# One core: local attention with the norm of z taken out of the ring, its normalisation on POOL, the reciprocals one step earlier, and a new order of the entry of layer 0

## The chip, the cores and the metric

The kernel runs on one NeuronCore of one Trainium2 chip. The metric is the time of one execution on the device in microseconds (us); lower is better. The engines are PE (TensorE: matrix products and transposes, results to PSUM), DVE (VectorE), ACT (ScalarE), POOL (GpSimd, which reads and writes SBUF only) and SP (SyncE, which issues the DMAs). Each engine runs its own instructions strictly in the order in which they are written; between engines there are only semaphores.

## The reference, cut to what matters

Two batches of 1024 tokens, 128 features. First a gated linear attention (chunks of 64), a norm and an addition; its output is normalised again and is the input of a transformer of two layers. The change lies in those layers, and in how the first of them begins beside the end of the linear attention. In each layer, for each token:

```python
h = shift_token(x)                      # half of the features taken from the token before
q, k, v = split(h @ wqkv)               # 8 heads of 64
q = l2norm(q) * qs ; k = l2norm(k) * ksc
q, k = rotary_xpos(q, k)
sim = q @ k.T                           # own window of 64 tokens and the one before, masked
o = softmax(sim) @ v
x = x + o @ wo
h = shift_token(x)
h = (h - mean(h)) / sqrt(var(h) + 1e-05) * lg + lb      # this is z
a, g = split(h @ w1 + b1)
x = x + (a * gelu(g)) @ w2 + b2
```

## The kernel before, in words

All tensors are float32, apart from the masks of the scores. The 2048 tokens are 16 tiles of 128 tokens (NT = 16; tiles n and n + 1 of a pair belong to the two batches). The linear attention works on 8 pairs of tiles (NP = 8). Its last four pairs run interleaved with the first tiles of layer 0; the order of this stretch is written out by hand for each engine in `attention_beside_last_pairs` (POOL L512, PE L1017, ACT L1434, DVE L1976). From tile FREE_TILE = 3 on, in layer 1 from tile 0 or 1 on, all engines run a loop `iterate(engine, step)`, in which a step k issues a fixed list of stages, each for the tile k + lag. These lists (`step` on POOL L507, `attn_step` on PE L981, ACT L1410 and DVE L1941) are the only thing that sets the order of the work, and four or five tiles are under way at once. A layer's end (`drain`) puts the last stages between the blocks of the feed-forward part, which takes groups of four tiles and needs their z.

For one tile the stages follow each other like this, over the engines:

- PE transposes the tile (L865), ACT copies it into h (L1334, L1335), PE projects q and k (`project_qk`, L867).
- DVE multiplies them by the rotary tables into rot1 and rot2 (`rotate`, L1857). ACT squares q and k (`squares`, L1342), DVE sums the squares (`sum_squares`, L1865) and bounds them from below (`bound_squares`, L1874), ACT takes ln and exp of them to the inverse norms (L1347, L1353).
- POOL adds the two halves of the rotation (`rotate_add`, L475) and scales by the inverse norms (`scale_qk`, L483). PE transposes the result (`transpose_qk`, L892), ACT copies it (`copy_qk_t`, L1361).
- PE computes the scores (`scores`), DVE takes the row maximum (`row_max`, L1885) and subtracts it (`subtract_max`, L1892), both in two halves of four heads, ACT takes the exponentials (L1367), PE transposes them (`transpose_probs`, L934), ACT copies them (`copy_probs_t`, L1374), PE multiplies by v (`weigh_values`), which also gives the row sums. v is projected by PE (`project_v`), copied by ACT (`copy_v_cur`, L1390), and POOL mixes it with the window before (`mix_values` L492, `keep_values` L503).
- DVE takes the reciprocals of the row sums (`row_reciprocals`, L1905) and normalises o with them (`normalise_o`, L1912). PE transposes o (`transpose_o`, L959), ACT copies it (L1381), PE projects it (`project_o`), DVE adds the input to `middle` (`add_attention`, L1919).
- SP shifts the tile by one token with three DMAs into `hcat` (L334 to L338). DVE takes its statistics (`stats_z`, `aggregate_z`, L1926, L1932), ACT ln and exp to the reciprocal deviation (`ln_of_z`, `rstd_of_z`, L1396, L1402), DVE normalises (`normalise_z`, L1938), PE transposes (`transpose_z`, L979), ACT scales it into z_t (`copy_z_t`, L1407). For the last two tiles of a layer, DVE and POOL do what ACT does here (L1960, L570), since ACT then holds the table for gelu.

`mv_z`, `ln_z` and `rstd_z` exist once, so `aggregate_z` of a tile waits for the normalisation of the tile before it (the semaphore zn_ready). `zn` exists twice, `hcat` four times.

## Time and profile before

| | before |
|---|---|
| median of 3 runs | 467.56 us (465.65 to 467.89) |
| the profiled execution: time, span | 466.54 us, 464.7 us |
| PE, weight load of PE | 417.9 us (90%), 293.2 us (63%) |
| DVE, ACT, POOL busy | 353.2 us (76%), 307.6 us (66%), 266.4 us (57%) |
| share of the chain that ended last | PE 30%, DVE 25%, ACT 20%, issue 14%, POOL 5%, DMA 1% |

The span is the time from the first to the last instruction of the profiled execution; its own time is 1.84 us more, and times worked out from the trace are compared with that execution and not with the median. Busy means that an instruction of the engine runs; waiting at semaphores does not count. The chain goes back from the last instruction, at each step to what released it or to the one before it on its engine. The order of the program in time: linear attention until about 85 us, mixed with the start of layer 0 from 76 us on; attention of layer 0 until 242 us; its feed-forward part with the start of layer 1 until about 285 us; attention of layer 1 until 424 us; the feed-forward part and the output norm until the end.

### The profile page before, as it was taken

What the parts mean: (1) busy time and instruction counts of PE and PEld (TensorE: products, weight loads), DVE (VectorE), ACT (ScalarE), POOL (GpSimd) and SP (SyncE); (2) the same over time, 40 slices, a digit from 0 to 9 for tenths busy, and PEclk for the clock granted to TensorE, in tenths of its full rate; (3) what the DMA queues carried; (4) which work ended last, traced back from release to release, by engine and by line L of the source; (5) the groups of instructions that cost most, each with busy time, mean ns of one, the idle gap of its engine ahead of it and who ended that gap; (6) DMA issues with size and microseconds to landing.
All of it is one profiled execution on the core that took longest, in us unless ns stands there. A gap on an engine that the chain in (4) does not pass through costs nothing.

```text
span 464.7 us, 13197 instructions
## 1 busy us (share of the span) xinstructions
PE 417.9 (90%) x4851; PEld 293.2 (63%) x4851; DVE 353.2 (76%) x750; ACT 307.6 (66%) x681; POOL 266.4 (57%) x253
## 2 busy tenths in 40 slices
PE   4898999787999999999879999899999999988994
PEld 2565666555667767666665566667767666765563
DVE  3688787886788888888754277888889888865666
ACT  3777868675678777877753247678777877766322
POOL 3578968997575666566450036564665556550134
PEclk9999999999899999999989999999999999999999
DMA  6910000000000000000000000000000000000012
GB/s 184 344 27 1 4 3 3 2 2 7 7 7 8 12 9 7 8 16 7 8 13 6 0 1 2 7 8 8 11 10 8 7 14 8 8 13 7 6 35 58
DMA packets 21038, 10.37 MB, mean 22 GB/s; under 512 B 13236, under 2 KB 20208, under 8 KB 20976
## 3 DMA queue, kind: packets, MB, share of 16 engines
q1 hardware_dynamic: 20400, 9.14, 7.2%
q8 instruction: 40, 0.66, 0.6%
q10 hardware_dynamic: 576, 0.39, 0.3%
q14 instruction: 22, 0.18, 0.1%
HBM read 6.38 MB, written 1.05 MB: 16 GB/s over the span
## 4 chain that ended last, share of the span: by engine, by line
PE 30%; DVE 25%; ACT 20%; issue 14%; POOL 5%; DMA 1%; SPq 1%; DVEq 0%; ACTq 0%; POOLq 0%
PE psum L620 25%; DVE ss L1865 7%; DVE neg_max L1885 7%; ACT sq L1342 6%; ACT qk_t L1361 5%; DVE probs L1892 4%; ACT probs_t L1374 3%; ACT probs L1367 2%; POOL qr L483 2%; PE psum L892 2%; ACT ln_z L1396 1%; DMA hcat<-middle 1%; DVE row_rec L1905 1%; POOL qr L475 1%; POOL ping L446 1%
## 5 line engine op out<-in xcount | busy, mean ns | idle before, releaser
L475 POOL TENSOR_TENSOR qr<-rot 128x1024 f32<-128x1024 f32 x32 | 75.9, 2371 | 75.7 <-issue 58.3
L620 PE MATMUL psum<-wqkv_sb,h_t 128*128 128x512 f32 x192 | 94.6, 603 | 0.6 <-ACT h_t L1335 0.6
L483 POOL TENSOR_TENSOR qr<-qr,inv 128x1024 f32<-128x1024 f32 x32 | 60.9, 1902 | 36.1 <-ACT inv L1353 36.0
L1865 DVE TENSOR_REDUCE ss<-sq 128x16 f32<-128x1024 f32 x32 | 39.0, 1217 | 27.6 <-ACT sq L1342 27.6
L1367 ACT ACTIVATE probs<-probs 128x512 f32<-128x512 f32 x64 | 40.4, 632 | 12.9 <-DVE probs L1892 12.2
L1892 DVE TENSOR_TENSOR probs<-psum,neg_max 128x512 f32<-128x512 f32 x64 | 44.0, 690 | 2.0
L620 PE MATMUL psum<-z_t,w_sb 128*128 128x512 f32 (+1 forms) x96 | 45.2, 604 | 0.0
L1885 DVE TENSOR_REDUCE neg_max<-psum 128x4 f32<-128x512 f32 x64 | 43.4, 681 | 1.0 <-PE psum L620 0.9
L620 PEld LDWEIGHTS psum<-wqkv_sb,h_t 128*128 128x128 f32 x192 | 31.8, 192 | 17.6 <-issue 16.7
L1857 DVE TENSOR_TENSOR rot<-psum,cos_t 128x1024 f32<-128x1024 f32 x32 | 38.8, 1213 | 4.0 <-PE psum L620 2.0
L892 PEld LDWEIGHTS psum<-consts,qr 128*128 128x128 f32 x256 | 29.8, 142 | 19.0 <-POOL qr L483 11.0
L1319 ACT ACTIVATE gelu<-psum,columns 128x512 f32<-128x512 f32 (+1 forms) x24 | 16.4, 685 | 36.1 <-PE psum L620 36.1
L1381 ACT ACTIVATE o_t<-psum 128x512 f32<-128x512 f32 x32 | 19.1, 596 | 30.3 <-PE psum L959 30.2
L1857 DVE TENSOR_TENSOR rot<-psum,sin_t 128x1024 f32<-128x1024 f32 x32 | 38.9, 1214 | 0.0
L620 PEld LDWEIGHTS psum<-v_mix,probs_t 128*64 128x64 f32 x512 | 32.6, 139 | 7.7 <-issue 4.3
L620 PE MATMUL psum<-v_cur,probs_t 128*64 128x65 f32 x512 | 37.1, 226 | 0.0
L620 PE MATMUL psum<-v_mix,probs_t 128*64 128x65 f32 x512 | 37.0, 226 | 0.1
L1836 DVE SCALAR_TENSOR_TENSOR hid<-psum,columns,gelu 128x512 f32<-128x512 f32 (+1 forms) x24 | 17.9, 748 | 24.6 <-ACT gelu L1319 24.6
L892 PE MATMUL psum<-consts,qr 128*128 128x128 f32 x256 | 33.6, 275 | 3.1 <-POOL qr L483 2.8
L1361 ACT ACTIVATE qk_t<-psum 128x1024 f32<-128x1024 f32 x32 | 32.8, 1025 | 4.5 <-PE psum L892 3.9
L1342 ACT ACTIVATE sq<-psum 128x1024 f32<-128x1024 f32 x32 | 33.0, 1032 | 3.8 <-DVE rot L1857 3.8
L620 PE MATMUL psum<-wo_sb,o_t 128*128 128x128 f32 x256 | 34.0, 276 | 1.4 <-ACT o_t L1381 1.4
(150 smaller groups left out, 954.2 us busy)
## 6 DMA issues: line engine op xcount, KB each, us to landing
wqkv_sb<-in_L_ffn_wqkv SPq DMA_DIRECT2D x1, 1536.0 KB, 9.5
hcat<-middle SPq DMA_DIRECT2D x32, 32.0 KB
out_x<-pong SPq DMA_DIRECT2D x8, 128.0 KB, 1.8
hcat<-middle SPq DMA_DIRECT2D x32, 31.8 KB
x_in<-in_L_attn_x SPq DMA_DIRECT2D x2, 384.0 KB, 4.4
w_sb<-in_L_ffn_w SPq DMA_DIRECT2D x1, 682.0 KB
cos_base<-rotary_cos SPq DMA_DIRECT2D x1, 512.0 KB, 5.0
sin_base<-rotary_sin SPq DMA_DIRECT2D x1, 512.0 KB, 6.0
```

Source lines behind the costliest of these rows:

```text
L475: pool.tensor_tensor(o, a, b[:, :, ::-1, :], ALU.add).then_inc(s["add_ready"], 1)
L483: pool.tensor_tensor(a, a, inv[:, :].unsqueeze(2).to_broadcast([P, 2 * AH, DH]), ALU.mult).then_inc(s["qr_ready"], 1)
L620: return pe.matmul(o, w, m, start=start, stop=stop, skip_group_check=skip)
L892: ins = pe.transpose(p_turn[:, c * P:(c + 1) * P], qr[:, at:at + P], ident)
L1342: act.activation(sq[:, :], p_qk[:, :], ACT.Square).then_inc(s["sq_ready"], 1)
L1361: act.activation(qk_t[:, at:at + 2 * INNER], p_turn[:, :], ACT.Copy).then_inc(s["qkt_ready"], 1)
L1367: act.activation(p, p, ACT.Exp).then_inc(s["p_ready"], 1)
L1381: act.activation(o_t[:, :], p_vo[:, :], ACT.Copy).then_inc(s["ot_ready"], 1)
L1857: ins = dve.tensor_tensor(o[:, :].rearrange("p (i h e) -> p i h e", i=2, e=DH), x, tab.unsqueeze(2).to_broadcast([P, 2, AH, DH]), ALU.mult)
L1865: dve.tensor_reduce(ss[:, 0:4 * AH:2], sq[:, :].rearrange("p (h e) -> p h e", e=DH), AX.X, ALU.add).then_inc(s["ss_ready"], 1)
L1885: dve.tensor_reduce(neg_max[:, a * PAIRS:(a + 1) * PAIRS], heads_of(p_sc, a), AX.X, ALU.max, negate=True).then_inc(s["max_ready"], 1)
L1892: dve.tensor_tensor(heads_of(probs, a, par * AH * P), heads_of(p_sc, a), neg_max[:, a * PAIRS:(a + 1) * PAIRS].unsqueeze(2).to_broadcast([ ...
```

## The change

The loop lists of the four engines, the normalisation of z and the ends of the layers:

```diff
@@ SP, the three DMAs of a tile @@
-                                 ).then_inc(d["d_half"], 16)
+                                 ).then_inc(d[("d_even", "d_odd")[n % 2]], 16)

@@ POOL @@
+                def normalise_z(n, par):
+                    N = base + n
+                    wait(pool, s["z_rstd"], N + 1)
+                    wait(pool, s["zt_done"], N - 1)
+                    pool.tensor_scalar(zn[:, par * P:(par + 1) * P], hcat[:, n % 4 * P:(n % 4 + 1) * P], mv_z[:, 0:1],
+                                       rstd_z[:, :], ALU.subtract, ALU.mult).then_inc(s["zn_ready"], 1)
+
                 def step(k, par):
                     staged(scale_qk, k, par, 1)
                     staged(mix_values, k, par, 0)
                     staged(keep_values, k, par, 0)
+                    staged(normalise_z, k, par, -3)
                     staged(rotate_add, k, par, 2)
...
                 iterate(pool, step, first=-1 if l else FREE_TILE, end=NT, before=parts)
 
+                pool.wait_ge(s["half_ready"], 1)
+                pool.wait_ge(s["vup_ready"], base + NT)
+                normalise_z(NT - 3, (NT - 3) % 2)
+                for n in (NT - 2, NT - 1):
+                    rstd_of_z(n)
+                    normalise_z(n, n % 2)
                 if l + 1 < DEPTH:
                     pool.wait_ge(s["rot_ready"], base + NT)
                     pool.wait_ge(s["vup_ready"], base + NT)
                     for i in range(4):
                         cos_part(l + 1, i)
                         sin_part(l + 1, i)
-                pool.wait_ge(s["half_ready"], 1)
-                pool.wait_ge(s["vup_ready"], base + NT)
-                for n in (NT - 2, NT - 1):
-                    rstd_of_z(n)

@@ PE, attn_step @@
                     staged(transpose_qk, k, par, 1)
+                    staged(transpose_probs, k, par, 0)
                     staged(project_o, k, par, -1)
-                    staged(transpose_probs, k, par, 0)
                     staged(project_v, k, par, 1)
+                    staged(weigh_values, k, par, 0)
                     staged(transpose_z, k, par, -3)
-                    staged(weigh_values, k, par, 0)

@@ ACT, attn_step @@
                     staged(exponentials, k, par, 0, 0)
                     staged(exponentials, k, par, 0, 1)
-                    staged(ln_of_z, k, par, -2)
-                    staged(rstd_of_z, k, par, -2)
                     staged(copy_qk_t, k, par, 1)
                     staged(copy_probs_t, k, par, 0)
                     staged(squares, k, par, 2)
                     staged(copy_v_cur, k, par, 1)
+                    staged(ln_of_z, k, par, -2)
+                    staged(rstd_of_z, k, par, -2)
                     staged(copy_z_t, k, par, -3)

@@ DVE @@
                 def stats_z(n, par):
                     N = base + n
-                    wait(dve, d["d_half"], 48 * (N + 1))
+                    wait(dve, d[("d_even", "d_odd")[n % 2]], 48 * (N // 2 + 1))
...
-                def normalise_z(n, par):
...
                 def attn_step(k, par):
-                    staged(row_reciprocals, k, par, -1)
                     staged(normalise_o, k, par, -1)
                     staged(row_max, k, par, 0, 0)
+                    staged(row_max, k, par, 0, 1)
                     staged(subtract_max, k, par, 0, 0)
-                    staged(row_max, k, par, 0, 1)
                     staged(subtract_max, k, par, 0, 1)
+                    staged(rotate, k, par, 2)
+                    staged(add_attention, k, par, -1)
                     staged(stats_z, k, par, -2)
                     staged(aggregate_z, k, par, -2)
-                    staged(rotate, k, par, 2)
-                    staged(normalise_z, k, par, -2)
-                    staged(add_attention, k, par, -1)
                     staged(sum_squares, k, par, 2)
+                    staged(row_reciprocals, k, par, 0)
                     staged(bound_squares, k, par, 2)
...
                 def normalised(n):
-                    for stage in (stats_z, aggregate_z, variance_z, normalise_z):
+                    for stage in (stats_z, aggregate_z, variance_z):
                         stage(n, n % 2)
...
                     def last_outputs():
-                        row_reciprocals(last, last % 2)
                         normalise_o(last, last % 2)

@@ attention_beside_last_pairs, one place of POOL and one of DVE @@
-                    normalise_f(4, 0)
-                    rotate_add(1, 1)
                     scale_qk(1, 1)
                     mix_values(0, 0)
                     keep_values(0, 0)
+                    normalise_f(4, 0)
                     normalise_f(5, 1)
+                    rotate_add(2, 0)
+                    scale_qk(2, 0)
+                    normalise_f(6, 0)
...
                     sum_squares(3, 1)
+                    bound_squares(3, 1)
+                    row_max(2, 0, 0)
+                    row_reciprocals(1, 1)
```

How this moves the instructions, at three places. DVE in the steady part of layer 0, before from the normalisation of z of one step to the statistics of the next, in the change from one sum of squares to the next (rot: rot1 and rot2; o_n: normalised o; neg_max: the row maxima; ss, ssc: sum and bounded sum of the squares). Before:

```order
L1938 TENSOR_SCALAR zn<-hcat,mv_z,rstd_z 128x128
L1919 TENSOR_TENSOR middle<-psum,ping 128x128
L1865 TENSOR_REDUCE ss<-sq 128x16
L1874 TENSOR_REDUCE ssc<-ss 128x16
L1905 RECIPROCAL row_rec<-psum 128x8
L1912 TENSOR_TENSOR o_n<-psum,row_rec 128x2x4x64
L1885 TENSOR_REDUCE neg_max<-psum 128x4
L1892 TENSOR_TENSOR probs<-psum,neg_max 128x512
L1885 TENSOR_REDUCE neg_max<-psum 128x4
L1892 TENSOR_TENSOR probs<-psum,neg_max 128x512
L1926 BN_STATS st_z<-hcat 128x6
L1932 BN_AGGR mv_z<-st_z 128x2
```

and in the change:

```order
L1874 TENSOR_REDUCE ss<-sq 128x16
L1914 RECIPROCAL row_rec<-psum 128x8
L1883 TENSOR_REDUCE ssc<-ss 128x16
L1921 TENSOR_TENSOR o_n<-psum,row_rec 128x2x4x64
L1894 TENSOR_REDUCE neg_max<-psum 128x4 x2
L1901 TENSOR_TENSOR probs<-psum,neg_max 128x512 x2
L1866 TENSOR_TENSOR rot<-psum,cos_t 128x1024
L1866 TENSOR_TENSOR rot<-psum,sin_t 128x1024
L1928 TENSOR_TENSOR middle<-psum,ping 128x128
L1935 BN_STATS st_z<-hcat 128x6
L1941 BN_AGGR mv_z<-st_z 128x2
L1874 TENSOR_REDUCE ss<-sq 128x16
```

The normalisation zn is gone from DVE, statistics and aggregation st_z and mv_z stand behind the addition to middle, the reciprocals row_rec between ss and ssc, and the two maxima come ahead of the two subtractions.

ACT in the same part, one step from the inverse norms inv on. Before:

```order
L1353 ACTIVATE inv<-ss_ln,columns 128x16
L1381 ACTIVATE o_t<-psum 128x512
L1334 ACTIVATE h_t<-psum 64x128
L1335 ACTIVATE h_t<-psum 64x128
L1367 ACTIVATE probs<-probs 128x512 x2
L1396 ACTIVATE ln_z<-mv_z,columns 128x1
L1402 ACTIVATE rstd_z<-ln_z 128x1
L1361 ACTIVATE qk_t<-psum 128x1024
L1374 ACTIVATE probs_t<-psum 128x512 x2
L1342 ACTIVATE sq<-psum 128x1024
L1390 ACTIVATE v_cur<-psum 128x8x64
L1407 ACTIVATE z_t<-psum,columns 128x128
```

and in the change:

```order
L1362 ACTIVATE inv<-ss_ln,columns 128x16
L1390 ACTIVATE o_t<-psum 128x512
L1343 ACTIVATE h_t<-psum 64x128
L1344 ACTIVATE h_t<-psum 64x128
L1376 ACTIVATE probs<-probs 128x512 x2
L1370 ACTIVATE qk_t<-psum 128x1024
L1383 ACTIVATE probs_t<-psum 128x512 x2
L1351 ACTIVATE sq<-psum 128x1024
L1399 ACTIVATE v_cur<-psum 128x8x64
L1405 ACTIVATE ln_z<-mv_z,columns 128x1
L1411 ACTIVATE rstd_z<-ln_z 128x1
L1416 ACTIVATE z_t<-psum,columns 128x128
```

ln_z and rstd_z stand ahead of the copy qk_t before, and behind the copy v_cur now.

DVE in the entry of layer 0, from the sum of squares of tile 3 to its bound and the following row maxima. Before:

```order
L1857 TENSOR_TENSOR rot<-psum,sin_t 128x1024
L1919 TENSOR_TENSOR middle<-psum,ping 128x128
L1865 TENSOR_REDUCE ss<-sq 128x16
L1926 BN_STATS st_z<-hcat 128x6
L1932 BN_AGGR mv_z<-st_z 128x2
L1874 TENSOR_REDUCE ssc<-ss 128x16
L1905 RECIPROCAL row_rec<-psum 128x8
L1912 TENSOR_TENSOR o_n<-psum,row_rec 128x2x4x64
L1885 TENSOR_REDUCE neg_max<-psum 128x4 x2
L1892 TENSOR_TENSOR probs<-psum,neg_max 128x512 x2
L1857 TENSOR_TENSOR rot<-psum,cos_t 128x1024
```

and in the change, from the same sum of squares to the statistics of z of tile 0:

```order
L1874 TENSOR_REDUCE ss<-sq 128x16
L1883 TENSOR_REDUCE ssc<-ss 128x16
L1894 TENSOR_REDUCE neg_max<-psum 128x4
L1914 RECIPROCAL row_rec<-psum 128x8
L1901 TENSOR_TENSOR probs<-psum,neg_max 128x512
L1921 TENSOR_TENSOR o_n<-psum,row_rec 128x2x4x64
L1894 TENSOR_REDUCE neg_max<-psum 128x4
L1901 TENSOR_TENSOR probs<-psum,neg_max 128x512
L1866 TENSOR_TENSOR rot<-psum,cos_t 128x1024
L1866 TENSOR_TENSOR rot<-psum,sin_t 128x1024
L1935 BN_STATS st_z<-hcat 128x6
L1941 BN_AGGR mv_z<-st_z 128x2
```

The statistics of z of tile 0 stood directly behind that sum, ahead of the bound; now they are the last but one row of the piece.

## Rows read from the trace of the kernel before

**Rows 1.** Windows: us, then busy (x count) by engine, PEclk granted, DMA share, GB/s.
```profile
106.00:117.00 11.00, 7.63 (x102) 5.58 (x101) 7.17 (x15) 6.50 (x14) 7.60 (x7) 1.00 0.03 7
117.00:127.10 10.10, 10.07 (x103) 6.77 (x103) 7.30 (x12) 6.26 (x13) 5.49 (x4) 0.83 0.03 7
181.38:226.62 45.24, 42.87 (x518) 31.23 (x518) 39.43 (x71) 34.55 (x73) 27.44 (x21) 1.00 0.04 9
```

**Rows 2.** Timeline of POOL, 127 to 410 us: start, duration, instruction, [idle before].
```profile
127.10 1.90 POOL L483 TENSOR_TENSOR qr<-qr,inv 128x1024 f32<-128x1024 f32 x1 [1.26 <-ACT inv L1353]
...
190.43 1.90 POOL L483 TENSOR_TENSOR qr<-qr,inv 128x1024 f32<-128x1024 f32 x1 [1.11 <-ACT inv L1353]
...
196.02 2.38 POOL L475 TENSOR_TENSOR qr<-rot 128x1024 f32<-128x1024 f32 x1 [2.30 <-issue]
...
226.62 1.90 POOL L483 TENSOR_TENSOR qr<-qr,inv 128x1024 f32<-128x1024 f32 x1 [1.11 <-ACT inv L1353]
...
292.49 1.90 POOL L483 TENSOR_TENSOR qr<-qr,inv 128x1024 f32<-128x1024 f32 x1 [1.15 <-ACT inv L1353]
...
410.11 1.90 POOL L483 TENSOR_TENSOR qr<-qr,inv 128x1024 f32<-128x1024 f32 x1 [1.11 <-ACT inv L1353]
```

**Rows 3.** Timeline of DVE, one steady period of layer 0.
```profile
188.26 1.22 DVE L1865 TENSOR_REDUCE ss<-sq 128x16 f32<-128x1024 f32 x1 [1.00 <-ACT sq L1342]
189.51 0.19 DVE L1874 TENSOR_REDUCE ssc<-ss 128x16 f32<-128x32 f32 x1
...
189.85 0.69 DVE L1912 TENSOR_TENSOR o_n<-psum,row_rec 128x512 f32<-128x512 f32 x1
190.46 0.68 DVE L1885 TENSOR_REDUCE neg_max<-psum 128x4 f32<-128x512 f32 x1
...
192.49 0.69 DVE L1892 TENSOR_TENSOR probs<-psum,neg_max 128x512 f32<-128x512 f32 x1
```

**Rows 4.** Timeline of ACT, the same period.
```profile
193.22 0.63 ACT L1367 ACTIVATE probs<-probs 128x512 f32<-128x512 f32 x1 [0.23 <-DVE probs L1892]
193.75 0.28 ACT L1396 ACTIVATE ln_z<-mv_z,columns 128x1 f32<-128x1 f32 x1
...
194.29 1.02 ACT L1361 ACTIVATE qk_t<-psum 128x1024 f32<-128x1024 f32 x1
...
196.24 1.03 ACT L1342 ACTIVATE sq<-psum 128x1024 f32<-128x1024 f32 x1
```

**Rows 5.** Timeline of PE, the same period.
```profile
189.89 0.33 PE L865 MATMUL psum<-consts,ping 128*128 128x128 f32 x1
190.59 0.65 PE L959 MATMUL psum<-consts,o_n 128*128 128x128 f32 x4 [0.37 <-DVE o_n L1912]
...
192.81 1.04 PE L892 MATMUL psum<-consts,qr 128*128 128x128 f32 x8
193.68 0.50 PE L620 MATMUL psum<-wo_sb,o_t 128*128 128x128 f32 x3
```

**Rows 6.** Timeline of DVE in the entry of layer 0.
```profile
115.46 0.29 DVE L1926 BATCH_NORM_STATS2 st_z<-hcat 128x6 f32<-128x128 f32 x1 [2.60 <-DMA hcat<-middle]
...
115.88 0.17 DVE L1874 TENSOR_REDUCE ssc<-ss 128x16 f32<-128x32 f32 x1
...
116.83 1.28 DVE L1885 TENSOR_REDUCE neg_max<-psum 128x4 f32<-128x512 f32 x2
118.02 1.28 DVE L1892 TENSOR_TENSOR probs<-psum,neg_max 128x512 f32<-128x512 f32 x2
```

**Rows 7.** Groups by line: engine, operation, tiles, shapes, count | busy us, mean ns | idle before.
```profile
L402 POOL TENSOR_SCALAR middle<-x_in,mv_x,rstd_x 128x128 f32<-128x128 f32 x16 | 14.2, 895 | 2.1 <-ACT rstd_x L1171 2.1
...
L1938 DVE TENSOR_SCALAR zn<-hcat,mv_z,rstd_z 128x128 f32<-128x128 f32 x32 | 11.5, 359 | 5.8 <-POOL rstd_z L570 3.0 <-ACT rstd_z L1402 2.8
```

**Rows 8.** Timeline of PE at the end of layer 1's attention.
```profile
421.73 0.66 PE L934 MATMUL psum<-consts,probs 128*128 128x128 f32 x4 [0.67 <-ACT probs L1367]
...
424.26 0.59 PE L620 MATMUL psum<-z_t,w_sb 128*128 128x512 f32 x1
```

More of the change, by code:

```diff
@@ L1056, in attention_beside_last_pairs @@
                     transpose_in(0, 0)
+                    key_values(6, 0)
+                    intra_outputs(6, 0)
                     state_outputs(6, 0)
@@ L1556, in attention_beside_last_pairs @@
                     copy_v_cur(3, 1)
+                    ln_of_z(0, 0)
+                    rstd_of_z(0, 0)
                 if l:
```

270 lines of the change are left out of this document (128 added, 142 removed).

## The prediction

> **What bounds the kernel now.** I read the stage windows first, to see where time is spent and whether an engine is full; then the starts of one repeated instruction, for the period of the ring; then one period engine by engine, to find which waits close it; last the entry, where the pace is irregular.
>
> The windows [rows 1] show PE busy 42.87 of 45.24 us in the steady part of layer 0, which is 8.58 us of each 9.05 us, and DVE 39.43. So PE is nearly full but not the bound. The period comes from the starts of POOL's scaling by the inverse norms, once per tile [rows 2]: 127.10 to 226.62 is 11 steps, 292.49 to 410.11 is 13 steps, each 9.05 us. These 24 steps are 217 of 464.7 us.
>
> What closes the ring is in [rows 3] and [rows 4]. Call S the start of the sum of squares (188.26). DVE goes on: bound at S+1.25, then reciprocals, normalisation of o at S+1.59, second subtraction S+4.23, its end S+4.92 (193.18). ACT starts the second exponential 0.04 later, then ln and rstd of z, then the copy of qk at S+6.03, and the squares of the next tile at S+7.98; they last 1.03, and the next sum of squares starts 0.04 after them, at S+9.05. Nobody on this round waits longer than a handoff, so it is the ring, and DVE's idle time of 1.00 us before each sum, which ends with the squares, is its result. From the end of the exponential (193.85) to the copy (194.29), 0.44 us go to the two ACT steps of z, in which PE's transposes of qk have long ended: they start at 192.81 and last 1.04 [rows 5].
>
> **The change in the ring, part by part.**
> - ln and rstd of z move behind the copy of v, where ACT next waits for DVE's bound of squares anyway. They leave the ring: up to 0.44 us.
> - The reciprocals go between the sum and the bound, which has to wait for the sum anyway (S+1.25 for a sum that lasts 1.22). The normalisation of o comes at about S+1.37 instead of S+1.59: 0.22 us. They now read the weighing of the same step; its last matmul comes just ahead of the scores of the next tile, and those are all issued before the transposition into h at S+1.63 (189.89, [rows 5]); 36 matmuls of scores before it, it is over when DVE comes to them.
> - Maximum, maximum, subtraction, subtraction. The entry already runs this order [rows 6]: from 116.83 to 119.30, 2.47 us, against 190.46 to 193.18, 2.72 us, in the ring [rows 3]. 0.25 us less. The first subtraction comes later than now, but ACT is still busy with the copies of o and h then, and the second exponential is the one on the ring.
> - The normalisation of z (0.36 us, [rows 7]) leaves DVE, and the statistics move behind the addition.
>
> With these, what is late next? The subtractions end at 1.37 + 3.08 = S+4.45, the second exponential at S+5.16. PE: the transposes of o start 0.74 after the normalisation, S+2.11; the transposes of qk 2.22 after those, S+4.33 (190.59 to 192.81, [rows 5]). POOL's scaling starts at S+2.17 (190.43, [rows 2]) and lasts 1.90, so it would allow S+4.12. The transposes end at S+5.37, ACT copies at S+5.40. From that copy to the next S it is 3.02 us as now (194.29 to 197.31). **Ring: 8.42 us.** The probabilities are now transposed straight after qk (S+5.20 to 6.2) and ACT copies them at S+6.4, so moving the projection of o behind them costs the ring nothing; without that move the copy would wait for PE by some 0.3 us.
>
> PE's own round is the second bound. Its 8.58 us hold the transposition into h (0.33 us long, followed by a wait of 0.37) that takes 0.11 us when something stands behind it (eight take 0.87, 192.81 to 193.68), so 8.36 us is the least. Two bounds 0.06 us apart disturb each other. I take **8.47 us**, a gain of 0.58 us; ends are 8.36 and 8.65 (the case below in which DVE's new order brings nothing). 24 x 0.58 = **13.9 us** (16.6 to 9.6).
>
> The normalisation of z on POOL: the nearest rows [rows 7] are 128x128 with two pointers, 0.895 us on POOL, against 0.359 us for the present one on DVE. It stands between keeping v and adding the rotation, where POOL idles 2.30 us (196.02, [rows 2]): from S+5.5 to S+6.4. DVE's aggregation needs it, and that comes behind the projection of o (S+6.07 to 7.13), the addition (0.3) and the statistics, at S+7.7, to end near S+7.9. It costs the ring nothing; if the cover of 1.3 us, and the 0.5 us that DVE then still has, went, the rival below is the price. The separate even and odd DMA semaphores add no instruction, and SP's order is the same.
>
> **The entry of layer 0.** DVE takes the statistics of z of tile 0 right behind the sum for tile 3 and waits 2.60 us for the DMA (115.46), with the bound of squares (115.88) queued behind it [rows 6]. It should have come at 112.9, so 3.0 us are lost. PE runs dry: 7.63 of 11.00 us, and then the granted clock is 0.83 over 117.0 to 127.1 [rows 1]: between the levels of 1.2 and 2.4 GHz, so part of this stretch ran at the lower after PE's wait. Relative to the pace of 9.05 the scaling of tile 4 at 127.10 is some 4.2 us late (stall 3.0, slow matmuls and refill 1.2, an estimate). The change puts the statistics behind the bound, two maxima, two subtractions and the rotation of tile 4: all 4.2 come back. Against that, the squares of tile 3 now wait for two copies of probabilities, 1.0 us. For it, POOL's four double normalisations of f move behind rotations and scalings (0 to 2.3 us), and one more interval runs at the new pace (0.6). Sum 3.8 to 6.1, with 2.8 as the end if the refill brings nothing; nearer the lower end, as PE and ACT are also full there: **4.5 us**.
>
> **The tails.** At the end of each layer the z of tile 13 is now late, and PE can only start the feed-forward after its transposition. Now [rows 8], from the second half of the turned probabilities (421.73) to the first feed-forward matmul (424.26), 2.53 us. Then, estimated from durations in [rows 4 to 7]: rest of the turning 0.43, projection of o 1.06, addition 0.36 (as long as the other 128x128 step of [rows 7]), statistics 0.42 (115.46 to 115.88), ln and rstd 0.54 (193.75 to 194.29), POOL 0.95, turning z 0.33 = 4.1 us, less 0.25 for the earlier subtraction: +1.3 us in layer 1, and in layer 0, where PE and DVE already have longer waits at this place, +0.1, which is a choice and not worked out (1.3 is its upper end). Tiles 14 and 15 add POOL's 0.9 for DVE's 0.35, once in PE's way per layer: +0.4 each. Together **+2.2 us** (1 to 3).
>
> **Sum.** The profiled execution took 466.54 us around a span of 464.7. 466.54 - 13.9 - 4.5 + 2.2 = 450.3. The median of the runs shown, 467.56, is 1.0 above it, so 451.3 as a median.
>
> **Rivals.**
> - DVE's order brings nothing. If each DVE instruction starts only when the one before has drained, independent neighbours are no quicker, and only ln and rstd of z leave: then the normalisation stays at S+1.59, PE's chain adds 0.22, and the period is 8.65. 24 x 0.40 = 9.6, time 455.6. Against it: [rows 6] show two maxima in 1.28 us where one lasts 0.68, so the second began 0.08 before the first ended. The Trainium skill ("VectorE: DVE Perf Modes", The DRAIN you can't avoid) says that the next op does not start until the pipe is empty and that the semaphore between chained ops costs nothing; by that rule this rival would hold, and the trace speaks against it.
> - PE becomes the bound, with waits of its own: the projection of o stands behind transposes that wait for exponentials, and scores come behind z's transposition. If 0.2 us of waits stay in its 8.58, the period is 8.8: 24 x 0.25 = 6.0, time 459.2. For it speaks that PE is full to 95%; against it that its wait for o (0.37) is just what gets shorter.
> - Slower: POOL's normalisation comes on the ring. DVE's aggregation of z waits for it, and the next sum of squares stands behind that. It decides from a POOL time of about 2.8 us on, and gives a loss from 3.4 us. At 4 us the period is 5.5 + 4.0 + 0.2 = 9.7, and 24 x 0.65 = 15.6 us are lost: 466.5 + 15.6 - 4.5 + 2.2 + 1.0 = 480.8. For it: POOL's idle time before the rotation's addition is put down to issue, so POOL might be held beside DVE. Against: 0.9 us in rows. The Trainium skill ("GPSIMD Engine Reference", Performance versus the Vector engine) keeps elementwise work on VectorE, about twice as fast; the rows, 0.895 to 0.359, agree, and on a path this would decide.
> - The ring shortens by under 0.15 us (a wait not seen), entry and tails cancel: 464 to 469.
>
> **How the numbers follow.** Forecast 0.75, DVE order 0.09, PE 0.10, POOL 0.03, cancelling 0.03. Low end: 466.54 - 16.6 - 6.1 + 1.0 + 1.0 = 445.8. High end: 466.54 - 9.6 - 2.8 + 3.0 + 1.0 = 458.1. Together 445.5 to 458. Over 0.5% (2.3 us, about what a measurement can tell from no change) faster: 0.94; within: 0.03; slower: 0.03.
>
> **What would show it.** Scaling starts 8.4 to 8.5 us apart; the copy of qk directly behind PE's transposes, not behind ACT work; the bound of squares before the normalisation of o by about 0.1 us; POOL's normalisation 0.8 to 0.9 us long and inside its former idle time; no DMA wait of DVE near tile 0 and a granted clock near 1.0 in the entry; PE waiting about 1 us for z at the start of each feed-forward. A period over 8.7, or an entry gain under 2 us, makes the forecast wrong.

## The result, and the profile after

The changed kernel takes **451.23 us** as a median of four runs (449.71 to 455.11), 0.9662 of the kernel before (95% interval 0.9585 to 0.9739). Five more runs of it gave 450.07 us (449.87 to 450.17), ratio 0.9642 (0.9605 to 0.9678). The execution profiled first happens to be the slowest of all nine: 455.11 us, span 453.3. A second one took 450.12 us, span 448.2. Both are used, since they differ mainly in one thing, the granted clock in the entry.

| stretch, by POOL's scaling starts | before | first | second | forecast | second against before |
|---|---|---|---|---|---|
| start to tile 4 of layer 0 (entry) | 127.10 | 127.25 | 122.11 | -4.5 | -4.99 |
| 11 + 13 steps of the ring | 217.14 | 202.84 | 202.85 | -13.9 | -14.29 |
| tile 15 of layer 0 to tile 2 of layer 1 | 65.87 | 66.92 | 66.97 | +2.2 | +1.10 |
| tile 15 of layer 1 to the end | 54.59 | 56.29 | 56.27 | (in the line above) | +1.68 |

All but the column of the forecast are us of the profiled executions; the last column is the second execution less the one before. The forecast's one term for the tails stands against 1.10 + 1.68 = 2.78 us. The four parts add up to -16.50 us, the difference of the spans 464.7 and 448.2. The rows are those of POOL in the second execution, which answer to [rows 2]:

```profile
122.11 1.90 POOL L483 TENSOR_TENSOR qr<-qr,inv 128x1024 f32<-128x1024 f32 x1 [1.01 <-ACT inv L1362]
...
173.02 1.90 POOL L483 TENSOR_TENSOR qr<-qr,inv 128x1024 f32<-128x1024 f32 x1 [0.48 <-ACT inv L1362]
...
176.42 0.79 POOL L511 TENSOR_SCALAR zn<-hcat,mv_z,rstd_z 128x128 f32<-128x128 f32 x1
...
215.28 1.90 POOL L483 TENSOR_TENSOR qr<-qr,inv 128x1024 f32<-128x1024 f32 x1 [1.06 <-ACT inv L1362]
...
391.93 1.90 POOL L483 TENSOR_TENSOR qr<-qr,inv 128x1024 f32<-128x1024 f32 x1 [1.06 <-ACT inv L1362]
```

The third row is the normalisation of z on POOL, 0.79 us long; POOL's addition of the rotation behind it, at 177.95, still waits 0.74 us for DVE, so it lies in idle time. Tiles 10 to 15 start from 173.02 to 215.28: four steps of 8.47 us and a last one of 8.36.

The windows show where the two executions part (columns as in [rows 1]); the first execution:

```profile
62.00:76.00 14.00, 13.23 (x179) 8.58 (x179) 9.54 (x28) 10.47 (x32) 10.76 (x13) 0.88 0.01 3
85.00:95.00 10.00, 9.01 (x121) 5.79 (x120) 7.51 (x15) 5.48 (x17) 7.85 (x7) 0.83 0.01 2
95.00:106.00 11.00, 8.39 (x73) 6.39 (x72) 8.08 (x20) 5.92 (x13) 9.68 (x10) 0.84 0.01 2
127.25:220.41 93.16, 93.16 (x1144) 68.79 (x1143) 82.35 (x143) 76.80 (x163) 71.74 (x59) 1.00 0.05 10
```

and the second:

```profile
62.00:76.00 14.00, 13.32 (x219) 9.17 (x215) 10.04 (x30) 11.27 (x34) 10.79 (x13) 1.00 0.01 3
85.00:95.00 10.00, 7.17 (x87) 4.66 (x82) 9.37 (x23) 6.50 (x19) 8.49 (x7) 1.00 0.01 2
95.00:106.00 11.00, 10.70 (x139) 7.57 (x140) 9.24 (x22) 7.21 (x20) 10.66 (x11) 1.00 0.01 2
122.11:215.28 93.17, 93.17 (x1144) 68.82 (x1143) 82.37 (x143) 76.75 (x163) 71.76 (x60) 1.00 0.05 10
```

In the entry the first has a granted clock of 0.88, 0.83 and 0.84 where the second has 1.00. The other runs of the change show the same: the mean clock was 0.983 in the one of 455.11 us, 0.989 in that of 452.47, and 0.993 or 0.994 in the seven of 449.71 to 450.17. The kernel before varies likewise, and more of its runs meet the low clock (10 of 17 had a mean of 0.991 or less). Against the seven of its runs that had 0.992 to 0.994 (464.91 to 466.03 us, middle 465.34), the gain is 15.3 us; the other 1.4 us of the 16.7 between the medians go with the clock. In the ring PE is busy all the time: 93.16 of 93.16 us, where [rows 1] had 42.87 of 45.24. PE is now the bound. The chain on the profile's page says the same: PE's share was 30% and is 69%.

One period of DVE in the second execution (answering to [rows 3]; S is 170.85):

```profile
170.85 1.22 DVE L1874 TENSOR_REDUCE ss<-sq 128x16 f32<-128x1024 f32 x1 [0.47 <-ACT sq L1351]
171.99 0.20 DVE L1914 RECIPROCAL row_rec<-psum 128x8 f32<-128x8 f32 x1
172.10 0.19 DVE L1883 TENSOR_REDUCE ssc<-ss 128x16 f32<-128x32 f32 x1
172.22 0.69 DVE L1921 TENSOR_TENSOR o_n<-psum,row_rec 128x512 f32<-128x512 f32 x1
173.12 1.29 DVE L1894 TENSOR_REDUCE neg_max<-psum 128x4 f32<-128x512 f32 x2 [0.21 <-PE psum L629]
...
178.14 0.29 DVE L1928 TENSOR_TENSOR middle<-psum,ping 128x128 f32<-128x128 f32 x1 [0.27 <-PE psum L629]
...
179.32 1.22 DVE L1874 TENSOR_REDUCE ss<-sq 128x16 f32<-128x1024 f32 x1 [0.47 <-ACT sq L1351]
```

of ACT:

```profile
175.04 1.23 ACT L1376 ACTIVATE probs<-probs 128x512 f32<-128x512 f32 x2 [0.23 <-DVE probs L1901]
176.37 1.02 ACT L1370 ACTIVATE qk_t<-psum 128x1024 f32<-128x1024 f32 x1
```

and of PE (answering to [rows 5]):

```profile
172.98 0.33 PE L874 MATMUL psum<-consts,ping 128*128 128x128 f32 x1
173.14 0.60 PE L968 MATMUL psum<-consts,o_n 128*128 128x128 f32 x4
173.58 1.88 PE L629 MATMUL psum<-wqkv_sb,h_t 128*128 128x512 f32 x4
175.30 1.04 PE L901 MATMUL psum<-consts,qr 128*128 128x128 f32 x8
```

The normalisation of o is at S+1.37, as forecast. The copy of qk (176.37) starts 0.03 us after PE's transposes of qk end (176.34) and 0.10 after the exponentials (176.27), so it follows directly on PE, as forecast. DVE has three short waits: 0.21 us for the scores, 0.27 for the projection of o, 0.47 for the squares. PE has none.

### The profile page after: what moved, and what is told of

It is laid out like the page before. It is cut to its first block, busy times and chain, and to the rows that moved or that the text cites. A ratio compares the mean times of both kernels' runs of the same rounds, so it can differ in the third digit from the quotient of the medians.

```text
span 453.3 us, 13199 instructions
## 1 busy us (share of the span) xinstructions
PE 418.1 (92%) x4851; PEld 295.6 (65%) x4851; DVE 339.3 (75%) x718; ACT 307.5 (68%) x681; POOL 291.5 (64%) x285
## 4 chain that ended last, share of the span: by engine, by line
PE 69%; issue 8%; DVE 4%; POOL 3%; ACT 3%; DVEq 0%; POOLq 0%; ACTq 0%
PE psum L629 51%; PE psum L901 6%; PE psum L943 6%; PE psum L968 3%; PE psum L988 2%; PE psum L874 1%; POOL qr L483 1%; POOL zn L511 1%; POOL rstd_z L578 1%; ACT probs_t L1383 0%; ACT sq L1351 0%; POOL ping L446 0%; PE psum L755 0%; ACT qk_t L1370 0%; DVE st_o L1792 0%
## 5 line engine op out<-in xcount | busy, mean ns | idle before, releaser
L1874 DVE TENSOR_REDUCE ss<-sq 128x16 f32<-128x1024 f32 x32 | 39.0, 1219 | 15.4 <-ACT sq L1351 15.3
L1376 ACT ACTIVATE probs<-probs 128x512 f32<-128x512 f32 x64 | 39.3, 631 | 12.1 <-DVE probs L1901 11.8
L1894 DVE TENSOR_REDUCE neg_max<-psum 128x4 f32<-128x512 f32 x64 | 41.4, 686 | 7.7 <-PE psum L629 7.6
L1901 DVE TENSOR_TENSOR probs<-psum,neg_max 128x512 f32<-128x512 f32 x64 | 41.1, 681 | 0.1
L943 PE MATMUL psum<-consts,probs 128*128 128x128 f32 x256 | 33.8, 274 | 4.2 <-ACT probs L1376 4.2
```

Of the source, the lines that this page charges most:

```text
L943: ins = pe.transpose(p_sc[:, a * 512 + c * P:a * 512 + (c + 1) * P], probs[:, at:at + P], ident)
L1376: act.activation(p, p, ACT.Exp).then_inc(s["p_ready"], 1)
L1874: dve.tensor_reduce(ss[:, 0:4 * AH:2], sq[:, :].rearrange("p (h e) -> p h e", e=DH), AX.X, ALU.add).then_inc(s["ss_ready"], 1)
L1894: dve.tensor_reduce(neg_max[:, a * PAIRS:(a + 1) * PAIRS], heads_of(p_sc, a), AX.X, ALU.max, negate=True).then_inc(s["max_ready"], 1)
L1901: dve.tensor_tensor(heads_of(probs, a, par * AH * P), heads_of(p_sc, a), neg_max[:, a * PAIRS:(a + 1) * PAIRS].unsqueeze(2).to_broadcast([ ...
```

## The experiments

Times are medians, and a ratio is that to the kernel before in the same series of runs. Period means the distance of two scaling starts in the middle of layer 0. S is the start of DVE's sum of squares in the step shown.

**1. The same kernel once more.** No edit.

> The changed kernel unaltered, for a second profiled execution. Theory A (the granted clock): the profiled execution of 455.11 us is the slowest of four, and its scaling of tile 4 starts at 127.25 us, no earlier than before, because the clock was granted at 0.83 to 0.88 in three windows of the entry (62:76, 85:95, 95:106). Then an execution near 450 us has a granted clock near 1.0 there, its tile 4 starts near 123 us, and its ring still has the period 8.47 (layer 0) and 8.44 us (layer 1). Theory B (the order): the reordered entry gains nothing whatever the clock. Then tile 4 starts at 127 again, and a faster execution is faster elsewhere. Time 451 us by both.

Measured: 450.07 us, tile 4 at 122.11, clock 1.00 in the windows above, periods 8.47 and 8.44. Theory A. The timelines of PE also show where the two executions part, first the slow one:

```profile
72.19 1.16 PE L629 MATMUL psum<-middle,wgk_sb 128*128 128x256 f32 x2 [0.26 <-ACT middle L1186]
73.14 3.16 PE L629 MATMUL psum<-wvg_sb,middle 128*128 128x512 f32 x4
76.14 1.03 PE L629 MATMUL psum<-middle,wqk_sb 128*128 128x256 f32 x4
```

then the other:

```profile
71.95 0.70 PE L629 MATMUL psum<-middle,wgk_sb 128*128 128x256 f32 x2 [0.26 <-ACT middle L1186]
72.48 1.88 PE L629 MATMUL psum<-wvg_sb,middle 128*128 128x512 f32 x4
74.20 1.03 PE L629 MATMUL psum<-middle,wqk_sb 128*128 128x256 f32 x4
```

The first of the same three groups starts 0.24 us apart in the two executions, the four matmuls then last 3.16 us against 1.88, and the next group is 1.94 us apart. Nothing in the program differs: the slow four ran at a granted clock of 0.57 (72 to 76 us), the others at 1.00. Two more such stretches (clock 0.50 between 90 and 92 us, and between 100 and 102) make it 5.14 us at tile 4. So the profiled execution of 455.11 us lost to the clock what the new entry gains.

**2. The loop without the entry, and the entry without the loop.** The first kernel has the change everywhere but in the four hand-written entry lists, which keep their old order; the second has the new order in these lists alone. One place of many:

```diff
 # loop_only: DVE, entry (old list)
                     sum_squares(3, 1)
+                    stats_z(0, 0)
+                    aggregate_z(0, 0)
                     bound_squares(3, 1)
```

> The new loop lists, the POOL normalisation and the new ends, with the entry of layer 0 in its old order. The forecast's terms: the entry is worth 4.5 us and is independent of the ring, so this takes 451.2 + 4.5, less 0.6 for the one interval at the new pace that counts in the entry = 455 us; period 8.47; DVE waits 2 to 3 us for the DMA of tile 0 again. Rival 1 (the entry is worth nothing, as the profiled execution of the change seems to say): 451 us. Rival 2 (the entry is worth more, since a stall is what lowers the clock): over 457 us.

> The old loop lists and old ends, with the entry of layer 0 in its new order (DVE normalises z). If the ring's 14.3 us come from the loop lists alone, the period is 9.05 us, and the time is 467.7 - 4.5 = 463 us. Rival 1 (the entry is worth nothing): 467.7 us. Rival 2 (the new entry starts the ring in a better phase): the period is under 9.0.

Measured: loop alone 456.8 us (454.3 to 458.47), ratio 0.9782 (0.9741 to 0.9823), period 8.47. Entry alone 461.69 us (459.42 to 466.58), ratio 0.9894 (0.9863 to 0.9924), period 9.05; its profiled execution, 466.58 us, had low clocks in the entry and is read for its period only. Expected were 455 and 463 us. The two halves give 10.0 and 5.1 us against 466.79, the whole 16.7. The profiled execution of the loop alone has clocks of 0.88, 0.84 and 0.83 in 62:76, 95:106 and 117:127, and runs of like mean clock account for the missing 1.6 us: five runs of the entry alone at 0.993 or 0.994 took 461.58 to 461.73 us, 3.7 under the 465.34 of before; two of the loop alone at 0.991 took 454.30 and 455.94, 11.7 under the two of before at 0.990 and 0.991 (466.54 and 467.03). Together that is 15.4 us, and the whole gives 15.3; but these are few runs. The entry's 4.5 us stand against 5.1 by the medians (3.5 to 6.4 by the interval) and 3.7 at like clock. The ring's period owes nothing to the way in which it is entered: it is 8.47 with the old entry and 9.05 with the new entry and the old lists. In the loop alone the stall is back:

```profile
119.28 0.29 DVE L1935 BATCH_NORM_STATS2 st_z<-hcat 128x6 f32<-128x128 f32 x1 [2.98 <-DMA hcat<-middle]
```

**3. Less work for PE.** PE projects a quarter of v only, for tiles 4 to 15 (the output leaves the rest of v out):

```diff
-                    mm(p_vo[:, :], h_cols(n), wl[:, 2 * INNER:3 * INNER]).then_inc(s["v_done"], 1)
+                    w_ = P if n >= 4 else INNER
+                    mm(p_vo[:, 0:w_], h_cols(n), wl[:, 2 * INNER:2 * INNER + w_]).then_inc(s["v_done"], 1)
```

> The change, in which PE projects only the first 128 of the 512 columns of v for tiles 4 to 15 of each layer (so the output leaves three quarters of v out). In the trace of the change the two matmuls of this projection show 1.02 us together (177.94 of the second profiled execution), and their next neighbour starts some 0.9 us later, so PE's round of 8.47 us gets about 0.65 us shorter. Theory A (PE closes the period): the period falls at once to what the ring allows. The forecast put the ring at 8.42 us; from the new trace, with the 0.21 us taken out that DVE waits for the scores, it is about 8.35. So 1.2 to 2.9 us faster in 24 steps, and DVE's wait before the row maxima is gone. Theory B (PE is merely full of waits that its modelled ends hide, and the ring closes the period at 8.47): the period stays at 8.47. Theory C (no ring near it): period 7.8, 16 us faster.

Measured: 449.42 us (448.36 to 450.1); the period is 8.35 (five steps from 172.43 to 214.19), theory A. The time hardly shows it (ratio 0.9638 against the change's 0.9642). By the spans the 24 steps take 2.1 us less (200.8 against 202.85), but from tile 15 of layer 0 to tile 2 of layer 1 it is 1.1 us more, and there the clock was at 0.57 over 216 to 220 us, where the second execution of the change had 1.00. The finding rests on the period. DVE:

```profile
170.25 1.22 DVE L1875 TENSOR_REDUCE ss<-sq 128x16 f32<-128x1024 f32 x1 [0.48 <-ACT sq L1352]
...
172.23 1.28 DVE L1895 TENSOR_REDUCE neg_max<-psum 128x4 f32<-128x512 f32 x2
...
178.61 1.22 DVE L1875 TENSOR_REDUCE ss<-sq 128x16 f32<-128x1024 f32 x1 [0.48 <-ACT sq L1352]
```

PE:

```profile
172.37 0.66 PE L969 MATMUL psum<-consts,o_n 128*128 128x128 f32 x4 [0.30 <-DVE o_n L1922]
...
174.58 1.04 PE L902 MATMUL psum<-consts,qr 128*128 128x128 f32 x8
```

and ACT:

```profile
174.14 1.23 ACT L1377 ACTIVATE probs<-probs 128x512 f32<-128x512 f32 x2
175.66 1.02 ACT L1371 ACTIVATE qk_t<-psum 128x1024 f32<-128x1024 f32 x1 [0.29 <-PE psum L902]
```

PE now waits (0.30 us for o), and so does ACT (0.29 us for the transposes of qk); DVE's wait before the maxima is gone. This is the ring without PE's round over it: transposes of o at S+2.12, of qk at S+4.33, copy at S+5.41, next S 2.95 later. The forecast had S+2.11, S+4.33, S+5.40 and 3.02 later. So the **ring is 8.35 us and PE's round 8.47**.

**4. Reciprocals behind the bound.**

```diff
                     staged(sum_squares, k, par, 2)
-                    staged(row_reciprocals, k, par, 0)
                     staged(bound_squares, k, par, 2)
+                    staged(row_reciprocals, k, par, 0)
```

> The change with the reciprocals behind the bound of squares again (of the same step). The forecast counted 0.22 us of the ring for them: the normalisation of o back at S+1.59. If the ring at 8.42 were all, the period would be 8.64 and the time +4 us. But PE closes the period at 8.47, and in its trace DVE waits 0.21 us for the scores just behind the normalisation, so most of it should be hidden: transposes of o at S+2.33 instead of S+2.29, period 8.47 to 8.52, 0 to +1.2 us. Rival (the order of these two brings nothing, drains decide): normalisation of o at S+1.37 as before and no change at all.

Measured: 455.51 us (453.23 to 458.47), period 8.57. My expectation was wrong: 0 to 1.2 us more, and it was 3.2 by the spans (451.4 against 448.2), all of it in the 24 steps. The profiled execution is the fastest of its four; the median lies 5.4 us above the change's, and what the other three lost beyond the 3.2 is open.

```profile
179.84 1.22 DVE L1874 TENSOR_REDUCE ss<-sq 128x16 f32<-128x1024 f32 x1 [0.48 <-ACT sq L1351]
...
181.43 0.69 DVE L1921 TENSOR_TENSOR o_n<-psum,row_rec 128x512 f32<-128x512 f32 x1
...
188.41 1.22 DVE L1874 TENSOR_REDUCE ss<-sq 128x16 f32<-128x1024 f32 x1 [0.48 <-ACT sq L1351]
```

The normalisation is at S+1.59, 0.22 us later, and 8.35 + 0.22 = 8.57: the whole 0.22 us is on the ring. I had subtracted DVE's wait of 0.21 us as if it were slack; it was only the difference of two bounds, and goes as soon as the ring is the longer one.

**5. ln and rstd of z ahead of the copy of qk; maximum and subtraction alternating; both.**

```diff
 # lnz_ahead, ACT (and the end of the list behind copy_v_cur)
+                    staged(ln_of_z, k, par, -3)
+                    staged(rstd_of_z, k, par, -3)
                     staged(copy_qk_t, k, par, 1)
 # max_sub, DVE
                     staged(row_max, k, par, 0, 0)
-                    staged(row_max, k, par, 0, 1)
                     staged(subtract_max, k, par, 0, 0)
+                    staged(row_max, k, par, 0, 1)
```

> The change with ln and rstd of z ahead of the copy of qk again, for the tile of the step before (so nothing waits for them). The forecast counted 0.44 us of the ring for them. In the change the exponentials end at S+5.42 and the copy starts at S+5.52, so the copy comes at about S+5.9, the period is 8.42 + 0.44 = 8.86 at most and 8.8 from the new trace, +8 to +9.4 us, and DVE waits 0.8 us for the squares. Rival (PE's round hides it, as it hides the reciprocals): under 8.55, under +2 us.

> The change with DVE's maximum and subtraction alternating again (maximum, subtraction, maximum, subtraction). The forecast credited the other order with 0.25 us of the ring. From the run with less projection of v: the exponentials ended at S+5.12 and PE's transposes of qk at S+5.38. With 0.25 us more the exponentials end at S+5.37, still inside, so the copy of qk does not move, and PE's round hides the rest: period 8.47, no change. Additive theory (each piece was worth what the forecast gave it, less the 0.11 us that PE hides): period 8.61, +3.4 us.

> The two earlier single edits together: ln and rstd of z ahead of the copy of qk (alone it made the period 8.51 to 8.62, mean 8.56), and maximum and subtraction alternating (expected alone: 8.47). Theory (a maximum of two paths): the exponentials end at S+5.37, 0.44 us for ln and rstd come behind them, copy at S+5.81, and 2.95 from the copy to the next S as in the run with less projection of v: period 8.76, so together they cost 0.29 us, where alone they cost 0.09 and 0.00. Additive theory: 8.56 plus what the alternation costs alone. The ends of the layers are as long as with the first edit alone (some 7 us more than in the change).

Measured periods: ln and rstd ahead 8.58 on the mean (8.51 and 8.66 in turn in layer 0, 8.55 and 8.62 in layer 1; the 8.56 in the third expectation was read too low), alternation 8.50, both 8.77. Times 461.72, 453.07 and 462.98 us, ratios 0.9891, 0.9737 and 0.9962; by their spans' parts the first and the third have 7.3 and 4.6 us in longer ends, where 7 were expected for both. There z of the last tiles comes a step later, but both profiled executions also have a low clock in layer 1's end, where the second execution of the change has 1.00 (0.57 over 412 to 416 us in the first, 0.62 over 420 to 424 in the third), and the two causes weren't separated. So these edits are judged by the period: each alone costs little (0.11 and 0.03 a step), both 0.30. ACT with both:

```profile
198.82 0.64 ACT L1376 ACTIVATE probs<-probs 128x512 f32<-128x512 f32 x1 [0.24 <-DVE probs L1901]
199.36 0.28 ACT L1405 ACTIVATE ln_z<-mv_z,columns 128x1 f32<-128x1 f32 x1
...
199.90 1.02 ACT L1370 ACTIVATE qk_t<-psum 128x1024 f32<-128x1024 f32 x1
```

Here the exponentials end at S+5.38 (S is 194.08), ln and rstd follow, and the copy comes at S+5.82 (expected 5.81), 0.41 us after that of experiment 3. With the two maxima in front the exponentials end at S+5.12, and PE's transposes, which end at S+5.38, cover more than half of ln and rstd; so alone these cost only 0.15 us of ring: 8.50, close to the shorter of the two periods in turn, 8.51. In the longer step the maxima start at S+2.12 (185.68, S is 183.56) and in the shorter at S+1.98 (177.03, S is 175.05); why the two take turns stays open. In the kernel before, ln and rstd were wholly on the ring because the maxima and subtractions alternated as well. The first expectation (8.8) missed this; the third, made with it, hit. The second was 0.03 too low. The alternation alone:

```profile
190.16 1.22 DVE L1874 TENSOR_REDUCE ss<-sq 128x16 f32<-128x1024 f32 x1 [0.62 <-ACT sq L1351]
...
192.29 0.69 DVE L1894 TENSOR_REDUCE neg_max<-psum 128x4 f32<-128x512 f32 x1
```

With PE as the bound the maxima wait for the scores and start at S+2.13, not S+1.98, so the exponentials end at S+5.54 (195.70) and no longer inside PE's transposes (S+5.37).

**6. The projection of o ahead of the transposes of the probabilities.** The two lines of PE's list exchanged.

> The change with PE's projection of o ahead of the transposes of the probabilities again. The forecast said that without this move the copy of the probabilities waits for PE by some 0.3 us. With the ring at 8.36: the transposes of the probabilities start at S+4.33+0.87+0.89 = S+6.09 and their first half is over at about S+6.7, where the copy can now start at S+6.32, so the squares and the next S come 0.35 us later: period 8.7, +5.5 us. Rival (PE's round of 8.47 us hides 0.11 us, and DVE's addition comes earlier and gives something back): period 8.5 or less, under 1 us.

Measured: 458.02 us, ratio 0.9851, period 8.83; expected was 8.7.

```profile
187.63 1.02 ACT L1370 ACTIVATE qk_t<-psum 128x1024 f32<-128x1024 f32 x1 [0.29 <-PE psum L901]
189.02 1.08 ACT L1383 ACTIVATE probs_t<-psum 128x512 f32<-128x512 f32 x2 [0.36 <-PE psum L943]
```

ACT waits 0.36 us, as expected, and the copy of the probabilities comes 1.39 us behind that of qk instead of 0.91 (175.66 to 176.57 in experiment 3): 0.48 us, the wait and the 0.11 us by which the two copies overlap when neither waits. 8.35 + 0.48 = 8.83. Without this line of the change 0.36 us a step would be lost, more than half of the ring's 0.58.

**7. z normalised on DVE; the last step in another order.** First the normalisation taken from POOL back to DVE; then the last step of each layer in another order; then the two together:

```diff
 # z_dve, DVE
                     staged(rotate, k, par, 2)
+                    staged(normalise_z, k, par, -3)
                     staged(add_attention, k, par, -1)
 # tail, DVE (and on ACT ln_of_z, rstd_of_z ahead of copy_qk_t in the last step)
-                    staged(add_attention, k, par, -1)
+                    if k < NT - 1:
+                        staged(add_attention, k, par, -1)
                     staged(stats_z, k, par, -2)
                     staged(aggregate_z, k, par, -2)
+                    if k == NT - 1:
+                        staged(add_attention, k, par, -1)
 # best: z_dve and tail (z of tile 13 normalised in the last step too), and on PE in that step
+                    staged(transpose_z, k, par, -3)
                     staged(weigh_values, k, par, 0)
```

> The change with the normalisation of z back on DVE, for the same tile as POOL does it, between the rotation and the addition to middle; all else in the new order. In the trace of the change DVE waits 0.27 us there for the projection of o and 0.47 us for the squares a little later, and the normalisation lasts 0.36 us. Theory (POOL's part in the gain is nil, only the place of the steps counts): period 8.47, and each layer's end gets back 0.4 us for z of tiles 13 to 15, so 0 to 1.5 us faster than the change. Rival (it had to leave DVE): 0.36 us come on the ring, period 8.6 to 8.8, +3 to +8 us.

> The change, with one step of each layer altered, the last one before the end: there ACT takes ln and rstd of z ahead of its copies, as before, and DVE takes the statistics of z ahead of the addition to middle. In the profile of the change, PE waits 1.07 us for POOL's normalisation just ahead of the feed-forward of layer 1 (412.52) and 0.64 us in layer 0 (237.00). If the late z of tile 13 is what this wait is made of, it goes, and the kernel gains 1 us in layer 1 and 0.3 to 0.6 us in layer 0: 449.8 us. Rival (z of tile 13 waits for the outputs of tile 13 and not for the order): PE waits for something else in the same place, and the time stays 451.2 us; the last tiles' own probabilities come 0.4 us later, up to 1 us slower.

> A candidate against both kernels: the ring as in the change, but z normalised on DVE (period 8.47 as before), and in the last step of each layer alone the statistics of z ahead of the addition, ln and rstd ahead of ACT's copies, and PE's transposition of z of tile 12 ahead of the weighing, so that the wait of 0.64 us for the copy of z_t behind it has something to stand beside. From the ends of the layers: 0.6 us each for the normalisation on DVE, 0.3 each for the transposition: 1.2 to 2.5 us under the change, 447.5 to 449 us where the clock is granted as in its second profiled execution. Rival (PE then waits in the same place for the addition of tile 14): 449.5 to 450 us. A stretch at the lower clock in the entry would add its 2 to 5 us in some executions, whatever these edits do.

Measured: z on DVE 451.37 us (447.57 to 453.94), period 8.47. DVE takes it where it waited for the projection of o:

```profile
186.17 0.34 DVE L1937 TENSOR_SCALAR zn<-hcat,mv_z,rstd_z 128x128 f32<-128x128 f32 x1
186.48 0.29 DVE L1918 TENSOR_TENSOR middle<-psum,ping 128x128 f32<-128x128 f32 x1
```

So nothing of the ring's gain needs POOL. What this run keeps of the change is the lag, z one step later; whether the lag was needed no run tests. The time shows no difference either way: the four runs lie between 447.57 and 453.94 us, ratio 0.9668 (0.9579 to 0.9757). From the scaling of tile 15 of layer 1 to the first feed-forward matmul: before 14.15 us, the change 15.69, z on DVE 15.21, other last step 15.23. The last step's order gave 0.46 us in layer 1 and not 1, and in layer 0 nothing (66.99 against 66.97 us to tile 2 of layer 1); the times, 449.64 us (449.43 to 451.47) against 450.07, are too close to tell apart. PE in this place, in the change:

```profile
407.45 0.33 PE L988 MATMUL psum<-consts,zn 128*128 128x128 f32 x1 [1.08 <-POOL zn L511]
407.62 0.60 PE L629 MATMUL psum<-z_t,w_sb 128*128 128x512 f32 x1
```

and with the other last step:

```profile
407.20 0.30 PE L988 MATMUL psum<-consts,zn 128*128 128x128 f32 x1 [0.64 <-ACT z_t L1416]
407.34 1.08 PE L629 MATMUL psum<-z_t,w_sb 128*128 128x512 f32 x2
```

The wait for z is replaced by one of 0.64 us for ACT's copy of the z before, since the transposed z has one place in PSUM. The combination, 448.38 us (447.96 to 451.54), has the ratio 0.9643 (0.9603 to 0.9683), the same as the change's 0.9642. The kernel before was also faster in that series (464.74 against 466.79 us), so the ratios count: the expected gain of 1.2 to 2.5 us isn't shown, and that 448.38 lies in the expected range confirms nothing. Its profile has the way shorter, 15.01 us in layer 0 (218.23 to 233.24) against 15.31 with z on DVE alone, which is the 0.3 us expected of the transposition. That execution met the low clock at another place:

```profile
226.23:230.23 4.00, 1.91 (x24) 1.32 (x17) 3.12 (x7) 2.26 (x6) 0.00 (x0) 1.00 0.02 4
230.23:234.23 4.00, 3.57 (x47) 2.74 (x46) 1.54 (x4) 2.27 (x6) 0.00 (x0) 1.00 0.05 12
400.93:404.93 4.00, 1.91 (x24) 1.32 (x17) 3.12 (x7) 2.26 (x6) 0.00 (x0) 1.00 0.02 4
404.93:408.93 4.00, 3.57 (x43) 3.08 (x41) 0.64 (x2) 1.50 (x4) 0.00 (x0) 0.57 0.04 8
```

The same four microseconds at the end of a layer, behind the same 2.09 us of waiting, ran at 1.00 in layer 0 and at 0.57 in layer 1. In the second execution of the change it is the other way about (0.58 in layer 0 from 227.28 on, 1.00 in layer 1), and with z on DVE neither fell. So the end of 56.77 us in the combination, against 55.65 with z on DVE alone, holds this stretch.

Three parts of the change were never undone alone: PE's weighing of v ahead of the transposition of z, the statistics of z behind DVE's addition, and the lag of the normalisation.

## Why the prediction was right

- **Time.** Its sum, 466.54 - 13.9 - 4.5 + 2.2, becomes 466.54 - 14.29 - 4.99 + 2.78 = 450.0, and the second execution took 450.12. The terms were off by 0.39, 0.49 and, the other way, 0.58 us, so that the sum came within 0.3 us is partly luck.
- **Period 8.47 us: right, with the two bounds exchanged.** "Ring: 8.42 us" was 8.35: the chain to the copy was right to 0.02, the rest, taken "as now" with 3.02 us, takes 2.95. "8.36 us is the least" for PE was 8.47. Against the 9.05 of before, PE's start of the transposition into h to that of o's transposes went from 0.70 us [rows 5] to 0.16 and the next distance from 0.50 to 0.44: 9.05 - 0.60 = 8.45, and the rest agrees within 0.02. The forecast took busy time less 0.22 as the round. It left out that the starts there are still 0.16 and not 0.11 apart, and that 8.58 us of modelled busy time and a wait of 0.37 don't yet make the 9.05 of the round. The added 0.05 for mutual disturbance has nothing to stand for: the longer bound simply holds. That it made up for the 0.11 missing from PE's round, and so gave 8.47, is luck. The second rival ("PE becomes the bound") thus happened as a mechanism, without its 0.2 us of waits and at 0.12 over the ring.
- **The rival "DVE's order brings nothing" did not come true.** Two maxima take 1.29 us, against 0.69 for one, and the normalisation of o is at S+1.37. The Trainium skill ("VectorE: DVE Perf Modes", The DRAIN you can't avoid) says that the next operation starts only with an empty pipe; by that two would take 1.38 us, an estimate from the 0.69. The same paragraph adds that an operation which isn't held starts earlier. The forecast's rival took only the first sentence; these rows agree with the second.
- **The pieces.** Reciprocals 0.22: right (experiment 4). "Up to 0.44" for ln and rstd and 0.25 for the order of the maxima: together 0.41 of the ring and not 0.69, because they lie on one of two parallel branches (experiment 5). The forecast's chain took the longer branch and so had this right; its list of pieces reads as if they added. 8.35 + 0.22 + 0.41 = 8.98; the missing 0.07 of 9.05 is the 3.02 against 2.95. It lies between the copy of qk and that of the probabilities, 0.98 us before (194.29 to 195.27) and 0.91 in experiment 3, so moving the projection of o probably gained it; the forecast had that move at nothing. That the pieces undone all at once give 9.05 again is a sum and not a run.
- **The projection of o** "costs the ring nothing; without that move the copy would wait for PE by some 0.3 us": the wait was 0.36 and the cost to the ring 0.48 (experiment 6).
- **POOL's normalisation** was forecast at 0.895, took 0.79 and costs the ring nothing; that the ring's period is the same with it on DVE, one step later, the forecast did not see.
- **Entry -4.5:** -4.99, and 5.1 by itself (3.7 at like clock, experiment 2). The DMA wait near tile 0 is gone. The execution of before has its own low stretch here (0.83 in [rows 1]), which the forecast counted into the 4.2 us. Not foreseen: a low clock in three stretches of some executions of the change. The mean clocks of the four first runs follow their spread of 5.4 us.
- **Tails +2.2:** +2.78. Layer 1: 1.3 + 0.4 forecast, 1.68 measured, but the parts are 1.54 us up to the first feed-forward matmul (15.69 against 14.15) and 0.14 behind it, so this hit too is partly luck. Layer 0: 0.1 + 0.4 forecast, 1.10 measured; the 0.1 was "a choice and not worked out", and up to the first feed-forward matmul it is 1.55 us (16.88 against 15.33). But both executions have a low clock in this place (0.57 over 240 to 244 us before, 0.58 over 227.28 to 231.28 in the change), the first from about that matmul on and the second ahead of it, so how much of either number is the late z isn't separated. Before the feed-forward PE waits 1.08 us for z in layer 1, as said. In layer 0 its wait is 0.64 us and is for ACT's copy of the z before, so the sign given for each feed-forward came true in layer 1 alone.

## What to carry to other kernels

When a loop is a ring between engines, write each branch as a chain of starts and take the longest, with every engine's own round as one more branch; savings that lie on parallel branches don't add, and undoing one of them tells less than it is worth. A wait seen on the engine that is second is the distance to the bound, not slack for the branch that runs through it. And where one profiled execution disagrees with the median of the runs, compare the granted clock window by window before doubting the change, and compare the tail of one kernel with that of another only where the clock is the same.

## What the runs showed of the hardware

- The granted clock fell to its lower level (1.2 of 2.4 GHz) in one execution and not in another of the same program, with the same groups only 0.24 us apart in time. Four matmuls of 512 columns took 3.16 against 1.88 us, the whole stretch around them cost 1.7 us (1.94 less 0.24), and three stretches in the entry made 5.14.
- Two DVE instructions that don't depend on each other overlap by 0.09 us (1.29 for two of 0.69); ACT's copy of the probabilities overlaps that of qk by 0.11 when it need not wait (175.66 + 1.02 against 176.57), and did not when it waited (experiment 6).
- PE's single transposition into h and the transposes of o behind it started 0.16 us apart with no wait between them (172.98 to 173.14), where eight transposes in a row take 0.11 each (175.30 to 176.17).
